# Six of the sixteen dense expert blocks summed by ScalarE and GpSimd, with the work around them put in another order

## What is computed

```python
# 1: cross attention; sim is normalised before its softmax
x = x + tanh(g_xattn[0]) * softmax(layernorm_affine(...), -1)
# 2: top-1 of 32 experts, each one masked ternary weight matrix
y = einsum('bsi,oi->bso', layernorm(x), w_scaled * mask_e)   # e = the row's expert
x = x + tanh(g_ffn[0]) * y * top1_w
# 3: keep the top 76 of each row of sim, sigmoid, symmetrise
A = sigmoid(sim) * (sim >= 76th largest of the row)
x = x + tanh(g_xattn[1]) * ((1 - gamma) * layernorm(x) + gamma * (A + A.T) / 2)
# 4: 64 gated experts with top 8 of them weighted, and one shared expert
inter = silu(x @ gate) * (x @ up) * W[:, e]
x = x + tanh(g_ffn[1]) * (sum over e of inter @ down_e + shared)
```

## Time and profile before

| | |
|---|---|
| median of 3 runs | 437.77 us |
| time of the profiled execution | 436.59 us |
| its span, first to last instruction | 434.8 us |
| mean granted TensorE clock | 0.952 of 2.4 GHz |
| TensorE busy | 392.1 us (90%) |
| VectorE busy | 313.3 us (72%) |
| ScalarE busy | 175.2 us (40%) |
| GpSimd busy | 103.2 us (24%) |

### The profile page before, as it was taken

How to read it: one execution, slowest core, us unless ns; L and a number is a source line. 1 busy time by engine, 2 the same in 40 slices (tenths; PEclk the granted TensorE clock), 3 DMA queues, 4 the chain that set the end, 5 groups by cost and what they waited for, 6 DMA issues and landing times. The chain is left out here.

```text
span 434.8 us, 7427 instructions
## 1 busy us (share of the span) xinstructions
PE 392.1 (90%) x2323; PEld 229.0 (53%) x2323; DVE 313.3 (72%) x787; ACT 175.2 (40%) x348; POOL 103.2 (24%) x126
## 2 busy tenths in 40 slices
PE   4997599899946999789999986999999999999995
PEld 1675146444534546345566654655565566655663
DVE  3689897999996768997996698566655555555554
ACT  2344977210226546345444533564223323333221
POOL 7603004531210604236345444300000000000000
PEclk9997599999988599999999997999999999999999
DMA  6999100373212054334455544102322112221221
GB/s 174 175 251 200 20 0 2 109 225 105 86 48 98 26 188 141 121 116 152 144 160 179 175 155 136 45 26 71 100 72 72 57 65 72 72 67 60 67 72 48
DMA packets 46520, 45.12 MB, mean 104 GB/s; under 512 B 6236, under 2 KB 37916, under 8 KB 46494
## 3 DMA queue, kind: packets, MB, share of 16 engines
q1 hardware_dynamic: 34108, 36.10, 26.9%
q0 software_dynamic: 8832, 5.24, 7.8%
q10 hardware_dynamic: 3554, 3.46, 2.5%
HBM read 42.03 MB, written 4.98 MB: 108 GB/s over the span
## 5 line engine op out<-in xcount | busy, mean ns | idle before, releaser
L995 PE MATMUL bank<-early,gu 128*128 128x512 f16 x768 | 177.0, 380 | 2.8 <-DVE arena L1615 2.6
L995 PEld LDWEIGHTS bank<-early,gu 128*128 128x128 f16 (+1 forms) x768 | 74.8, 98 | 82.7 <-issue 5.8
L479 ACT ACTIVATE arena<-arena 128x512 f16<-128x512 f32 (+1 forms) x66 | 41.6, 630 | 146.5 <-DVE arena L1629 138.6
L1019 PE MATMUL bank<-dp,arena 128*128 128x256 f16 (+1 forms) x768 | 95.5, 275 | 5.7 <-DVE arena L1639 5.7
L1019 PEld LDWEIGHTS bank<-dp,arena 128*128 128x128 f16 x768 | 75.2, 99 | 29.2 <-DVE arena L1639 8.4
L1615 DVE TENSOR_TENSOR arena<-arena,bank 128x512 f32<-128x512 f32 (+1 forms) x66 | 45.0, 684 | 47.8 <-PE bank L995 34.9
L1639 DVE TENSOR_TENSOR arena<-arena 128x512 f16<-128x512 f32 (+1 forms) x66 | 46.9, 711 | 35.6 <-ACT arena L479 35.6
L890 PE MATMUL bank<-gu,arena 128*128 128x512 f16 x256 | 59.2, 387 | 1.3 <-ACT arena L479 1.3
L416 POOL TENSOR_TENSOR gu<-stage,gu 128x512 f16<-128x512 f32 x32 | 39.1, 1221 | 78.4 <-ACT dp L479 78.4
L1629 DVE TENSOR_TENSOR arena<-arena,early 128x512 f32<-128x512 f32 x64 | 48.8, 762 | 7.5 <-DVE arena L1615 2.7
L676 ACT ACTIVATE arena<-bank 128x512 f32<-128x512 f32 (+1 forms) x66 | 38.7, 587 | 16.7 <-PE bank L995 16.6
(11 more groups left out here) (192 smaller groups left out, 346.1 us busy)
## 6 DMA issues: line engine op xcount, KB each, us to landing
early<-token_weights SPq DMA_DIRECT2D x126, 128.0 KB, 2.9
stage<-in_gu_t SPq DMA_DIRECT2D x32, 256.0 KB, 2.7
gu<-in_masks_t POOLq DMA_DIRECT2D x16, 256.0 KB, 24.0
stage<-in_dp_t SPq DMA_DIRECT2D x32, 128.0 KB, 2.8
dp<-gu SPq DMA_DIRECT2D x15, 128.0 KB, 2.5
routed_rows<-arena SPq DMA_DIRECT2D x1, 1536.0 KB, 18.4
arena<-routed_rows ACTq DMA_DIRECT2D x4, 384.0 KB, 5.4
expert_rows<-arena ACTq DMA_DIRECT2D x6, 256.0 KB, 2.1
```

Source lines behind the costliest of these rows:

```text
L479: return nc.scalar.activation(dst, src, ACT.Copy, scale=scale)
L995: last = mm(dst[0:m, :], w, x16[:, h, b, c, :], start=(k == 0), stop=(k == 3 * C - 1))
L1019: last = mm(dst, inter16[0:m, s, a, k * P:(k + 1) * P], w, start=(q is None and j == 0 and k % 2 == 0), stop=True, skip_group_check=True)
```

## The change

ScalarE takes blocks 8 to 13 out of PSUM (`scaled`): it multiplies each half of the bank by its row weight and writes it to `part`, which is the unused space of `Z` for half 1. GpSimd adds the two halves to `Z` (`add_parts`), and then scales the tile and adds it to `X` as before. VectorE keeps blocks 0 to 7, 14 and 15. GpSimd also makes the low halves of half 0's rows (`low_rows`), which `sort_rows` did on VectorE.

The order changes with it. VectorE does `adjacency` ahead of the last two blocks. TensorE does `symmetric(0)` ahead of the routed experts, and `prep_x3t(0)` ahead of the last piece of them. `mix_rows(0)` stands ahead of `expert_rows(2)` on ScalarE. The DMAs to `expert_rows` are issued by SyncE. Four more pairs of weights (6 to 9) are loaded and converted ahead of the loop, so that step n converts pair n + 8 and the last one is done in step 23. In half 0's loop `prep_x3t(1)` and `prep_rows(1)` move from step 26 to 27, `prep_logits(1)` from 27 to 28, `top_find(1)` and `top_rows(1)` from 28 to 29, and `top_weigh(1)` from 29 to 30. `low_step` stays on VectorE.

```diff
+        SHARED = range(2 * HT, 2 * HT + 2 * (HT - 1))
+        OWN = [i for i in range(DENSE) if i not in SHARED]
+        part = Z[:, HT:T, :].rearrange("p (s m) d -> p s m d", s=2)
...
-            load_pair(2)
-            load_pair(3)
+            for q in range(2, 6):
+                load_pair(q)
             load_spares()
-            load_pair(4)
-            load_pair(5)
+            for q in range(6, 10):
+                load_pair(q)
+            for p in range(PIECES):
+                sp.wait_ge(y_copied, p + 1)
+                sp.dma_start(y_v[:, 2 * p:2 * p + 2, :], ys[:, 2 * p:2 * p + 2, :]).then_inc(y_out, 16)
...
+                if n < PAIRS - 10:
+                    load_pair(10 + n)
...
+            def low_rows(t):
+
+                pool.wait_ge(hi16_ready, t + 1)
+                nc.gpsimd.tensor_tensor(rows16[:, t % HT, 1, :], XN[:, t, :], rows16[:, t % HT, 0, :],
+                                        ALU.subtract).then_inc(rows_ready if t >= HT else lo16_ready, 1)
+
+            def add_parts(t, j):
+
+                n = 2 * t + j
+                pool.wait_ge(sum_free, n + 1)
+                if j == 0:
+                    pool.wait_ge(dense_free, HT + t + 1)
+                else:
+                    pool.wait_ge(part_added, n)
+                m = steps(nc.gpsimd.tensor_tensor(Z[:, t, :], Z[:, t, :], part[:, n % 2, 0, :], ALU.add))
+                steps.need(m)
+                nc.gpsimd.tensor_tensor(Z[:, t, :], Z[:, t, :], part[:, n % 2, 1, :], ALU.add).then_inc(part_added, 1)
+
...
             rsqrt(1, HT)
             rsqrt(2, HT)
+            for t in range(HT):
+                low_rows(t)
+            low_half(0)
+            low_half(1)
             rsqrt(3, HT)
             for t in range(HT, T):
...
-            scatter()
+                low_rows(t)
             low_half(2)
             low_half(3)
+            scatter()
+            low_half(4)
+            low_half(5)
             pool.wait_ge(late_in, 16 * 4)
             for t in range(HT - 1):
-                pool.wait_ge(dense_free, 2 * (t + 1) + 2 * HT)
-                m = steps(nc.gpsimd.tensor_tensor(Z[:, t, :], Z[:, t, :], scale_sb[:, :], ALU.mult))
-                steps.need(m)
-                nc.gpsimd.tensor_tensor(X[:, t, :], X[:, t, :], Z[:, t, :], ALU.add).then_inc(rows_added, 1)
+                add_parts(t, 0)
+                if t == 2:
+                    low_half(6)
+                    low_half(7)
+                add_parts(t, 1)
+                add_rows(t)
             rsqrt(4, HT)
             rsqrt(5, HT)
-            low_half(4)
-            low_half(5)
+            low_half(8)
+            low_half(9)
             gather()
-            for q in range(6, 13):
+            for q in range(10, PAIRS):
                 low_half(q)
-            rsqrt(6, HT)
-            for q in range(13, 28):
-                low_half(q)
+                if q == 16:
+                    rsqrt(6, HT)
             rsqrt(7, HT)
-            for q in range(28, PAIRS):
-                low_half(q)
...
-                act.wait_ge(y_copied, p + 1)
-                act.dma_start(y_v[:, 2 * p:2 * p + 2, :], ys[:, 2 * p:2 * p + 2, :]).then_inc(y_out, 16)
+
+            def scaled(i):
+
+                bp, k = ORDER[i]
+                n = i - SHARED[0]
+                act.wait_ge(dense_ready, i + 1)
+                act.wait_ge(x1_ready, T)
+                if n >= 2:
+                    act.wait_ge(part_added, n - 1)
+                for j in range(2):
+                    last = copy(part[:, n % 2, j, :], ps_dense[i % 4][:, j * D:(j + 1) * D],
+                                c_mem[:, k, 2 * bp + j:2 * bp + j + 1])
+                last.then_inc(sum_free, 1)
...
             router_rows(0)
+            high_half(0)
+            high_half(1)
             norm_rows(0)
             router_exp(0)
...
             tanh_rows(0)
+            for i in SHARED:
+                scaled(i)
+                if i == 2 * HT + 4:
+                    high_half(6)
+                    high_half(7)
             routed_rows(0)
             routed_rows(1)
-            for p in range(PIECES):
+            for p in range(PIECES - 1):
+                if p == 2:
+                    mix_rows(0)
                 expert_rows(p)
                 if p + 2 < PIECES:
                     routed_rows(p + 2)
-                if p == 2:
-                    mix_rows(0)
 
...
             prep_rows(0)
-            high_half(4)
-            high_half(5)
+            expert_rows(PIECES - 1)
+            high_half(8)
+            high_half(9)
...
-                if n - 2 < PAIRS - 6:
-                    high_half(6 + n - 2)
+                if n + 8 < PAIRS:
+                    high_half(n + 8)
                 if n == 4:
                     tanh_rows(1)
                 if n == 10:
                     mix_rows(1)
-                if n == 26:
+                if n == 27:
                     prep_rows(1)
-                if n == 28:
+                if n == 29:
                     top_rows(1)
...
-                    pe.wait_ge(dense_free, i - 3)
+                    if i - 4 in SHARED:
+                        pe.wait_ge(sum_free, i - 3 - SHARED[0])
+                    else:
+                        pe.wait_ge(dense_free, OWN.index(i - 4) + 1)
...
                 if p < 2:
-                    pe.wait_ge(dense_free, DENSE - 3 + p)
+                    pe.wait_ge(sum_free, DENSE - 3 + p - SHARED[0])
...
-            experts(0)
-            routed_x(2)
-            experts(1)
-            routed_x(3)
             symmetric(0)
-            for p in range(2, PIECES):
+            for p in range(PIECES - 1):
                 experts(p)
                 if p + 2 < PIECES:
                     routed_x(p + 2)
             prep_x3t(0)
+            experts(PIECES - 1)
             prep_logits(0)
...
-                if n == 26:
+                if n == 27:
                     prep_x3t(1)
-                if n == 27:
+                if n == 28:
                     prep_logits(1)
...
-                dve.wait_ge(hi16_ready, t + 1)
-                v.tensor_tensor(rows16[:, t, 1, :], XN[:, t, :], rows16[:, t, 0, :], ALU.subtract).then_inc(lo16_ready, 1)
...
-            for i in range(6, DENSE - 1):
-                dense_rows(i, 2)
-                if i in (12, 14):
-                    rows_stats(i // 2 - 6)
-                find(4)
+            dense_rows(6, 2)
+            dense_rows(7, 2)
+            left = HT * (2 * ROUNDS - 1) - used[0]
+            find(left // 3)
+            rows_stats(0)
+            find(left // 3)
+            rows_stats(1)
+            find(left - 2 * (left // 3))
+            for t in range(HT):
+                adjacency(t)
+            find(3)
+            dense_rows(DENSE - 2, 2)
             rows_stats(2)
-            find(max(0, HT * (2 * ROUNDS - 1) - used[0]))
+            find(3)
             dense_rows(DENSE - 1)
             rows_scale(0, HT - 1)
             rows_add(HT - 1)
             rows_var(HT - 1)
-            for t in range(HT):
-                adjacency(t)
+            rows_sym(0, 0)
             rows_affine(0)
-            find(2)
-            rows_sym(0, 0)
             rows_sym(0, 1)
             rows_mix(0)
             rows_moments(0)
```

More of the change, by code:

```diff
@@ L628, in _ @@
             grouped(3)
-            high_half(0)
-            high_half(1)
+            high_half(2)
+            high_half(3)
             router_rows(1)
@@ L634, in _ @@
             sim1_rows(1, 0, 1)
-            high_half(2)
-            high_half(3)
+            high_half(4)
+            high_half(5)
             act.wait_ge(row_out, 16 * HT)
```

38 lines of the change are left out of this document (18 added, 20 removed).

## The result

| | before | after |
|---|---|---|
| median of 4 runs each, side by side | 437.64 us (437.45 to 439.95) | 427.92 us (427.22 to 428.85) |
| time and span of the profiled execution | 436.59, 434.8 us | 427.94, 426.2 us |
| mean granted TensorE clock | 0.952 | 0.964 |
| TensorE, VectorE busy | 392.1, 313.3 us | 387.2, 310.9 us |
| ScalarE, GpSimd busy | 175.2, 103.2 us | 179.7, 114.9 us |

The ratio of after to before is 0.9769, with a 95% interval of 0.9748 to 0.9791: 2.3% faster. The forecast was 428.0 us.

What follows compares the result with a forecast made beforehand. TensorE bounds the second half of the gated experts, so idle time ahead of it counts. 3.8 us (place one) plus 6.0 us (place two) gave 9.8 us off 437.77 us, forecast 428.0 us, range 424.8 to 433.5 us.

Steps and rivals of the forecast that it cites:

- What bounds the kernel: TensorE alone bounds the second half of gated experts, so moving that half's start moves the end by as much.
- Place two: Steps 25 to 27 of half 0's loop: TensorE's wait for XN goes, 6.0 us less, bounds 3.5 and 7.0.
- Rival 2: The loop's stall only moves one step, so only 3.8 us are gained: 434.0 us; chance 0.12.
- The request: VectorE's request for the inverse deviation, ahead of mix: 0.7 us later, near 127.3, with 0.8 us for adjacency beside GpSimd.
- Rival 1: GpSimd's adds hold VectorE, adjacency loses all 3.2 us: 430.4 us; chance 0.10.
- `XN` and behind it: Half 0: mix_rows(0) starts at 129.4 instead of 133.40, so XN comes 4.0 us earlier; 3.8 us taken as gain.
- rival 3: TensorE's clock returns early between the transposes of XN and the shared step: 1.5 us more, 426.5 us; chance 0.15.
- The lower end, 3.1: Gain with the clock still low at XN: 4.0 us less 0.9 us for experts(5) ahead of the logits.
- The shared blocks: VectorE up to the request: six dense blocks go (3.1 us), adjacency and two search steps come; net -0.1 us.
- place one: 119 to 146 us, from the dense blocks' end, with TensorE idle and its clock low: 3.8 us gained, 3.1 to 5.3.
- Edits costed at nothing: Early copies, low_rows beside GpSimd's low halves (up to 2 us without ScalarE's cover) and SyncE's DMAs: no cost.
- Rival 4: Load behind high_half(6) lands late on ScalarE; each us beyond the 3.4 us cover is lost, 445.9 us; chance 0.06.

Runs made afterwards that it cites:

- move_only: Kernel before, with only half 0's loop calls for transposes of XN, copies, logits and top-eight search put one step later; 438.97 us, ratio 1.0028.
- pairs_before_spares: Changed kernel with SyncE's loads of pairs 6 and 7 put ahead of the 15 DMAs of load_spares; 423.18 us, ratio 0.9704.
- mix_first: Kernel before, with only ScalarE's mix_rows(0) put ahead of expert_rows(2); 434.32 us, ratio 0.9912.
- both_loads: Changed kernel with loads of pairs 6 and 7 ahead of the spares, and of pairs 10 and 11 ahead of the token weights; 421.87 us, ratio 0.9647.
- scalar_delay: Changed kernel with 20 idle copies on ScalarE ahead of the conversion of pair 6; 428.18 us, ratio 0.9776.
- adj_behind_request: Changed kernel with adjacency put behind the request for the deviation, and symmetric(0) ahead of experts(4); 425.40 us, ratio 0.9682.

## Why the prediction was right, and where it was not

**What bounds the kernel** held: behind step 29 both kernels take 152.6 to 152.7 us, and every us won ahead of it came through. That the median came within 0.1 us of the forecast is partly luck. The spans differ by 8.6 us and not by the 9.8 of the sum. The forecast added 1.2 us, because the profiled execution of before lay that far under its median, and the profiled one of after lay at its median. The same changed kernel had 426.54 us in the second batch.

**Place two** (6.0 forecast, 6.1 measured) went by its steps: the wait of 1.49 us at step 25 stayed, `rows_normalise(1)` fell to 1.37 us, the transposes waited for nothing, and the logits 0.81 us where 1.0 was worked out. Rival 2 did not come. `move_only` shows that it is the real course once GpSimd is still busy: the stall moves one step and keeps its price. The prediction's reason against it (the long instruction loses its partner) is what decides: 3.77 us in `move_only`, 1.37 to 1.38 wherever GpSimd was done.

**The request** was forecast 9.1 us behind the last dense block (127.3 - 118.2) and came at 9.20. The sum was right, but two of its terms were off. `adjacency` cost 1.7 us more than alone, not 0.8, so the rest of VectorE's list must have been some 0.8 us shorter than the working of 0.52 us a block had it. Rival 1 in full (3.2 us) did not come either. The Trainium skill (SBUF — State Buffer, Who interferes with whom) says that a VectorE instruction with two SBUF inputs contends with a GpSimd one that reads SBUF, and calls the ports that they share an exclusive lock. The trace agrees: the four instructions of VectorE took 0.79, 0.94, 0.94 and 0.94 us, together 3.38 instead of 1.67; the last three began some 0.1 us behind one of GpSimd each, and those three took 0.78 to 0.79 instead of 0.73. So each is held once, by one of GpSimd's, and not by the run of four, as L1400 was in the earlier trace rows, an instruction of another kind (TENSOR_SCALAR). That costs about half of the bound of 3.2 us and not a quarter. `pairs_before_spares` shows the term by itself: without the partner 1.65 us, and the request 1.7 us earlier.

**`XN` and behind it.** `XN` gained 4.1 us (forecast 4.0; its transposes began 21.68 us behind the last dense block before and 17.59 after). The step that failed is the 0.7 us taken between 3.1 and 3.8 for an early return of the clock, and with it rival 3's price of 1.5 us on top. In the first profile the clock stayed low through the shared step (5.18 us against 4.75 before). In the second it returned in the logits, and TensorE waited 2.18 us for VectorE's weights of the experts, a chain that the prediction didn't look at. The lower end, 3.1, was too high as well: 2.7 us were gained with the low clock, and 2.3 with the early one. One profile of before is a weak base here too. `move_only`, whose program is the same up to step 25, took 36.62 us for the stretch that took 37.91 in the first. Against that base the gain is 1.1 to 1.5 us.

**The shared blocks** were worked out at nothing (-0.1 us net) for VectorE. In the changed kernel that held, as `mix_first` shows. But the working had the wrong reason: it made the blocks cheap on VectorE. In fact their gain was there (the request came 7.49 us behind the last dense block with `adjacency` undisturbed, and 8.35 before), and `adjacency` beside GpSimd spent it. With the last additions out of the way place one took 31.2 and 31.4 us (`pairs_before_spares` and `both_loads`), 3 us less than `mix_first`. Both sides had the early clock in their profiles.

**Edits costed at nothing.** The start was not nothing: counted from the router's first matmul it gained 1.2 us (0.7 from the span's start, since the two profiles differ by 0.5 us ahead of that mark). The held VectorE instructions were foreseen (the two of `diag` took 2.10 us, where each takes 0.69 in the kernel before), and the cover did not hold: the start of gathering came 0.8 us later. But the shorter gap gave 0.8 us and the clock 1.3, more than that. The loop's loss of 0.9 us is mostly the wait for one load, which the order of before has too. The prediction followed SyncE's queue to pair 6 and 9, but not to pair 10, which stands behind the write and read back of the token weights and in front of a SiLU, and whose wait the change left as it was.

**Rival 4** did not decide. Its cover was given as 3.4 us and measured 3.1 us. `scalar_delay` has its rule right for `XN`, and not for the time: 0.3 to 1.6 us were lost, with 4.8 us of delay. Its chance was put by the landing time of 2.7 us alone. The larger risk was when the load could be issued, and `adj_behind_request` shows 3 us of that by chance.

## What to carry over

A stall that is moved one step later is only hidden when its cause ends; otherwise the next user in the chain waits, and the same edit is worth -0.7 or +2.8 us. Where two engines hold each other up, look at the transfers that decide when the second one runs, before moving the work: with two loads moved ahead in a DMA queue the work already handed to GpSimd began to pay, 3.4 us. And take an early clock for a gain only when what comes behind is ready too. Before a loss or a gain of 1 us in one stretch is put down to a change, look at a second profile of the same program.

## What the hardware did that was not expected

- Later can be faster. With the gathers of half 0 starting 0.8 us later behind the router's matmuls, and a gap of 0.52 us behind them where 1.33 stood, TensorE's granted clock was at or near 2.4 GHz in the first dense block (0.94 in the changed kernel, 0.50 before; 1.9 to 2.2 us for 8 matmuls and not 3.4 to 3.6). The gap and the clock together gave 2.1 us back. What makes the chip grant it was not separated from that gap, which stood with it each time.
- The same program had TensorE's clock low or full through the shared step (5.18 or 2.78 us) in two executions, while the times differ by 2.4 us, most of it elsewhere (the wait for pair 10, which one of them had and the other not).
- Two copies of ScalarE out of PSUM took 0.82 to 0.84 us together while GpSimd and VectorE were at work, and 0.82 us while GpSimd was idle (from 92.55 us in the changed kernel): nothing held them.
